# Feature sums and key-value sums in column tiles of 32, running states ahead of the linear masks

## The reference

```python
x = x + attn_a(layernorm(x), ...)   # stage a: 16 heads of 64
x = x + ffn(layernorm(x), ...)      # 16 experts, the best 8, and a shared one
x = x + attn_b(layernorm(x), ...)   # stage b: 6 transformer layers, 16 heads of 8
x = x + ffn(layernorm(x), ...)
```

```python
SK = jnp.cumsum(ok, axis=2) + SK_state[:, :, None]   # ok: kk (outer) vk, per token
norm = jnp.sqrt(jnp.sum(SK * SK, axis=(-2, -1), keepdims=True)) + 1e-08
y = jnp.einsum('bhni,bhnji->bhnj', q, SK / norm)
```

```python
kv = jnp.einsum('bhclm,bhcld->bhcmd', Kc, Vc)        # keys times values, per chunk
num = scores @ Vc + Qc @ (cumsum(kv) - kv)           # scores: masked Qc Kc^T
den = scores.sum(-1) + Qc @ (cumsum(ksum) - ksum)
```

## Time and profile before

| | |
|---|---|
| Time, median of 3 runs | 3790.42 us (3784.97 to 3793.73) |
| Time of the profiled execution | 3792.82 us |
| Its span, first to last instruction | 3791.1 us |
| Mean granted TensorE clock, share of full speed | 0.974 |
| Busy: PE, PEld | 3495.8 us (92%), 2727.7 us (72%) |
| Busy: DVE, ACT, POOL | 2686.2 us (71%), 1684.5 us (44%), 902.1 us (24%) |

### The profile page before, as it was taken

One profiled execution on the slowest core, in us unless ns is written; L12 is line 12 of the kernel. 1 busy time (PEld: TensorE's weight loads), 2 busy tenths in 40 slices (PEclk: granted clock), 3 DMA queues, 4 the chain that ended last, 5 costly groups with the idle time before them and its releaser, 6 DMA issues. The chain is left out here.

```text
span 3791.1 us, 98421 instructions
## 1 busy us (share of the span) xinstructions
PE 3495.8 (92%) x39640; PEld 2727.7 (72%) x39640; DVE 2686.2 (71%) x6838; ACT 1684.5 (44%) x3438; POOL 902.1 (24%) x781
## 2 busy tenths in 40 slices
PE   4999999999999999799948999999999999977998
PEld 3777777777777777688836777777777777756887
DVE  3666666666666666588866888878888888857787
ACT  2555555555555555433324444444444444423332
POOL 3222233222232322100002322332232223320000
PEclk9999999999999999899979999999999999988999
DMA  2000000000000000000000000000000000000000
GB/s 87 28 25 30 23 28 28 23 28 24 29 25 28 23 24 25 8 1 1 0 15 16 2 16 3 2 16 2 16 2 3 16 2 3 2 2 1 1 1 23
DMA packets 38361, 59.71 MB, mean 16 GB/s; under 512 B 6960, under 2 KB 16688, under 8 KB 37552
## 3 DMA queue, kind: packets, MB, share of 16 engines
q1 hardware_dynamic: 37936, 53.78, 4.2%
HBM read 18.10 MB, written 2.10 MB: 5 GB/s over the span
## 5 line engine op out<-in xcount | busy, mean ns | idle before, releaser
L661 ACT ACTIVATE a_prob<-a_s,a_shift,a_scale 128x128 f32<-128x128 f32 (+3 forms) x512 | 312.1, 614 | 531.1 <-DVE a_shift L744 531.1
L1541 ACT ACTIVATE ffn_silu<-ffn_ps_g 128x512 f32<-128x512 f32 x272 | 161.3, 599 | 383.5 <-PE ffn_ps_g L1491 371.6
L1484 PEld LDWEIGHTS ffn_ps_y<-moe_down,ffn_hidden 128*128 128x128 f32 x2176 | 282.1, 191 | 41.3 <-issue 19.9
L1484 PE MATMUL ffn_ps_y<-moe_down,ffn_hidden 128*128 128x128 f32 x2176 | 288.1, 275 | 17.4 <-DVE ffn_acc L1645 17.4
L943 POOL TENSOR_TENSOR t_rstd<-t_var_eps,minus_half 128x4 f32<-128x4 f32 x96 | 97.7, 1018 | 821.7 <-DVE t_var_eps L1255 821.7
L1193 ACT COPY t_num<-t_n 128x512 f32<-128x512 f32 x96 | 56.3, 586 | 517.9 <-PE t_n L1004 517.4
L1645 DVE SCALAR_TENSOR_TENSOR ffn_acc<-ffn_ps_y,ffn_combine,ffn_acc 128x128 f32<-128x128 f32 x960 | 269.4, 343 | 7.6 <-PE ffn_ps_y L1484 0.5
L1657 DVE TENSOR_TENSOR ffn_hidden<-ffn_silu,ffn_ps_u 128x512 f32<-128x512 f32 x272 | 185.1, 682 | 108.6 <-ACT ffn_silu L1541 74.6
L1330 DVE TENSOR_TENSOR t_mixed<-t_s,upto 128x512 f32<-128x512 f32 x384 | 238.1, 682 | 17.0 <-PE t_s L980 15.2
L408 POOL TENSOR_TENSOR a_k_sin<-a_k_swap,sin_swap 128x512 f32<-128x512 f32 x64 | 81.5, 1274 | 661.6 <-DMA a_k_swap<-a_k_own 661.6
L741 DVE TENSOR_REDUCE a_neg_max<-a_s 128x2 f32<-128x256 f32 (+3 forms) x256 | 208.8, 816 | 32.0 <-PE a_s L560 30.1
(11 more groups left out here) (209 smaller groups left out, 8777.3 us busy)
## 6 DMA issues: line engine op xcount, KB each, us to landing
a_k_swap<-a_k_own SPq DMA_DIRECT2D x128, 128.0 KB, 2.1
a_y_swap<-a_y_own SPq DMA_DIRECT2D x128, 128.0 KB, 2.0
a_staged<-in_pairs SPq DMA_DIRECT2D x8, 384.0 KB, 2.9
t_next<-in_t_w SPq DMA_DIRECT2D x12, 256.0 KB, 2.9
t_next_rows<-in_t_rows SPq DMA_DIRECT2D x6, 448.0 KB, 3.9
x<-in_x SPq DMA_DIRECT2D x8, 256.0 KB, 4.9
out<-x SPq DMA_DIRECT2D x1, 2048.0 KB, 8.7
t_next_sq<-in_t_sq SPq DMA_DIRECT2D x6, 256.0 KB, 2.5
```

Of the source, the lines that this page charges most:

```text
L661: nc.scalar.activation(prob[c % 2][h][:, 0:(c + 1) * P], ps[f"s{h}"][:, 0:(c + 1) * P], ACT.Exp, bias=shift[:, k:k + 1], scale=scale[slot. ...
L1484: t = nc.tensor.matmul(ps_y[e % 2][:, c * P:(c + 1) * P], hidden[e % 3][:, c * P:(c + 1) * P], w_down[:, e * P:(e + 1) * P], start=True, s ...
```

## The change

Four edits are made.

1. In stage a the step St moves ahead of L1 in DVE's order. PE's order, in which St already stands ahead of L1, stays.
2. The step inc is cut into column tiles: each of its 4 matmuls becomes 4, with 32 stationary columns each, written to 4 groups of 32 partitions.
3. In stage b the step sums is cut the same way: each of 8 matmuls with 128 stationary columns and 144 (or 72) streamed ones becomes 4 with 32 stationary columns and 36 (or 18) streamed ones, the 2 heads whose features those 32 columns are. All of it now fits in bank w0, and w1 is no longer used for it.
4. DVE's part follows: one copy and three adds on 72 (the last on 36) elements form the running sums in `k_sum`, from PSUM, and then two multiplications by `own_head` spread them into `kv`. Before, two such multiplications came first, from PSUM, and three adds on 288 (the last on 144) elements followed in `kv`.

The rest of the change is the declaration of the semaphores `k_sums` and `kv`, which replace `kv_sum`.

```diff
--- before.py
+++ after.py
@@ -215,7 +215,7 @@
     SLOT = ("P0 T3 S0 P1 W3 inv P2 S1 L0 outs T0 P3 weights T1 St L1 Xn S2 W0 W1 Yi Ys T2 S3 W2 inc").split()
     LEAD = "X P0 P1 P2 L0 P3 L1 Xn St Yi Ys inc".split()
     ACT = "P0 T3 S0 P1 inv P2 S1 T0 P3 T1 S2 Ys T2 S3".split()
-    DVE = "W3 S0 inv S1 L0 outs P3 weights L1 S2 St Ys S3 inc rot scale".split()
+    DVE = "W3 S0 inv S1 L0 outs P3 weights St L1 S2 Ys S3 inc rot scale".split()
     FILLS = dict(X="", Xn="", Yi="", P0="a0 a1", P1="a2 a0", P2="a1 a2", L0="a0 a1", P3="a0 a1", St="a2", L1="a0 a1",
                  Ys="a0 a1", inc="a2", inv="t0", outs="a2", T0="t0", weights="", T1="t1", T2="t0 t1", T3="t0 t1",
                  **{f"S{c}": "s0 s1" for c in range(TILES)},
@@ -523,8 +523,10 @@
                         wait(pe, "zk_sums", slot, 1)
                         free("a2")
                         for c in range(TILES):
-                            t = nc.tensor.matmul(ps["a2"][:, 2 * c:2 * c + 2], zk_upto[:, c * P:(c + 1) * P],
-                                                 mem["twos_own"][:], start=True, stop=True)
+                            for r in range(4):
+                                at = c * P + 32 * r
+                                t = nc.tensor.matmul(ps["a2"][32 * r:32 * (r + 1), 2 * c:2 * c + 2],
+                                                     zk_upto[:, at:at + 32], mem["twos_own"][:], start=True, stop=True)
                         t.then_inc(filled["a2"], 1)
                     elif step == "inv":
 
@@ -769,7 +771,7 @@
     END = "att Wo h1 F1 F2".split()
     DVE = "values Wo Wo_norm mapk keys weights F1 sums S0 F2 nums F2_norm S1".split()
     WITH = dict(Wo_norm="Wo", F2_norm="F2")
-    FILLS = dict(weights="", turn="w0", project="w1 w0", values="n1", mapq="s0 s1", mapk="s2 s3", keys="w0 w1", sums="w0 w1",
+    FILLS = dict(weights="", turn="w0", project="w1 w0", values="n1", mapq="s0 s1", mapk="s2 s3", keys="w0 w1", sums="w0",
                  S0="s0 s1 s2 s3", S1="s0 s1 s2 s3", A0="n0", A1="n1",
                  nums="w0 n1", att="n0", Wo="n0", h1="n0", F1="s0 s1 s2 s3", F2="w1")
 
@@ -792,7 +794,7 @@
     L, H, D, FEAT, FT = 6, 16, 8, 16, 4
     V = D + 1
     EPS = 1e-6 * FEAT
-    HALF = H // 2 * V
+    PAIR = 2 * V
     SPAN, SPANS = P // 2, 2 * TILES
     PAD = 16
     ROOT = float(D) ** -0.25
@@ -834,6 +836,7 @@
         k_tok = sb("k_tok", [P, 2, TILES, P])
         v_tok = sb("v_tok", [P, TILES, 2, H, V])
         v_pad = sb("v_pad", [P, SPANS, H // 2, 2, PAD])
+        k_sum = sb("k_sum", [P, 2, SPANS - 1, PAIR])
         kv = sb("kv", [P, SPANS - 1, H, PAD])
 
         mixed = [[sb(f"mixed{t}_{r}", [P, SPANS, SPAN]) for r in range(4)] for t in range(2)]
@@ -988,7 +991,7 @@
                     bank = f"n{t}"
                     if t == 0:
                         wait(pe, "v_pad", slot, 1)
-                        wait(pe, "kv_sum", slot, 3)
+                        wait(pe, "kv", slot, 2)
                     wait_free(pe, bank, slot, f"A{t}")
                     for r in range(4):
                         wait_free(pe, f"s{r}", slot, "A0" if t == 0 else slot.steps[0])
@@ -1057,17 +1060,20 @@
                     elif step == "sums":
 
                         wait(pe, "v_tok", slot, 1)
-                        for t_, bank in enumerate(("w0", "w1")):
+                        for bank in ("w0", "w1"):
                             ready(bank, "keys")
-                            free(bank)
+                        free("w0")
+                        for t_ in range(2):
                             for c in range(TILES):
                                 n = 2 if c < TILES - 1 else 1
-                                t = nc.tensor.matmul(
-                                    ps[bank][:, 2 * c * HALF:(2 * c + n) * HALF].rearrange("p (s n) -> p s n", s=n),
-                                    k_tok[:, t_, c, :],
-                                    v_tok[:, c, 0:n, 8 * t_:8 * t_ + 8, :].rearrange("p s h d -> p s (h d)"),
-                                    start=True, stop=True)
-                            t.then_inc(filled[bank], 1)
+                                at = (t_ * (SPANS - 1) + 2 * c) * PAIR
+                                for r in range(4):
+                                    t = nc.tensor.matmul(
+                                        ps["w0"][strip(r), at:at + n * PAIR].rearrange("p (s n) -> p s n", s=n),
+                                        k_tok[:, t_, c, strip(r)],
+                                        v_tok[:, c, 0:n, 8 * t_ + 2 * r:8 * t_ + 2 * r + 2, :]
+                                        .rearrange("p s h d -> p s (h d)"), start=True, stop=True)
+                        t.then_inc(filled["w0"], 1)
                     elif step == "S0":
 
                         wait(pe, "kz", slot, 2)
@@ -1292,24 +1298,25 @@
                             nc.vector.tensor_copy(k_tok[:, t_, :, :].rearrange("p c n -> p (c n)"),
                                                   ps[bank][:]).then_inc(emptied[bank], 1)
                     elif step == "sums":
-                        for t_, bank in enumerate(("w0", "w1")):
-                            full(bank)
+                        full("w0")
+                        new = ps["w0"][:, 0:2 * (SPANS - 1) * PAIR].rearrange("p (t s n) -> p t s n", t=2, n=PAIR)
+                        nc.vector.tensor_copy(k_sum[:, :, 0:2, :], new[:, :, 0:2, :]).then_inc(s["k_sums"], 1)
+                        for c in range(1, TILES):
+                            wait(dve, "k_sums", slot, c)
+                            at = slice(2 * c, min(2 * c + 2, SPANS - 1))
+                            n = at.stop - at.start
+                            t = nc.vector.tensor_tensor(k_sum[:, :, at, :], new[:, :, at, :],
+                                                        k_sum[:, :, 2 * c - 1:2 * c, :].broadcast_to([P, 2, n, PAIR]),
+                                                        ALU.add)
+                            t.then_inc(s["k_sums"] if c < TILES - 1 else emptied["w0"], 1)
+                        wait_emptied(dve, "w0", slot, "sums")
+                        for t_ in range(2):
                             nc.vector.tensor_tensor(
-                                kv[:, :, 8 * t_:8 * t_ + 8, 0:V],
-                                ps[bank][:, 0:(SPANS - 1) * HALF].rearrange("p (c h n) -> p c h n", c=SPANS - 1, h=8),
-                                mem["own_head"][:].rearrange("p (h n) -> p h n", h=8).unsqueeze(1)
-                                .broadcast_to([P, SPANS - 1, 8, V]),
-                                ALU.mult).then_inc(emptied[bank], 1)
-
-                        wait_emptied(dve, "w0", slot, "sums")
-                        wait_emptied(dve, "w1", slot, "sums")
-                        for c in range(1, TILES):
-                            if c > 1:
-                                wait(dve, "kv_sum", slot, c - 1)
-                            sums = kv[:, 2 * c:min(2 * c + 2, SPANS - 1), :, 0:V]
-                            n = sums.shape[1]
-                            nc.vector.tensor_tensor(sums, sums, kv[:, 2 * c - 1:2 * c, :, 0:V]
-                                                    .broadcast_to([P, n, H, V]), ALU.add).then_inc(s["kv_sum"], 1)
+                                kv[:, :, 8 * t_:8 * t_ + 8, 0:V].rearrange("p u (r h) n -> p u r h n", r=4),
+                                k_sum[:, t_, :, :].rearrange("p u (h n) -> p u h n", h=2).unsqueeze(2)
+                                .broadcast_to([P, SPANS - 1, 4, 2, V]),
+                                mem["own_head"][:].rearrange("p (r h n) -> p r h n", r=4, h=2).unsqueeze(1)
+                                .broadcast_to([P, SPANS - 1, 4, 2, V]), ALU.mult).then_inc(s["kv"], 1)
 
                         if "A1" in slot.steps:
                             wait_filled(dve, "n1", slot, "A1")
```

More of the change, by code:

```diff
@@ L857, in transformer_block @@
         emptied = {k: sem("emptied_" + k) for k in plan.BANKS}
-        EVENTS = dict(o_now=1, o_bias=1, kz=4, kv_sum=3, v_tok=1, v_pad=1, den=2, inv=2,
+        EVENTS = dict(o_now=1, o_bias=1, kz=4, k_sums=3, kv=2, v_tok=1, v_pad=1, den=2, inv=2,
                       stats=8, mv=8, eps=2, rstd=2, xn=8, scaled=2, h1b=1, o_new=1)
-        PHASE = {n: "in" if n in ("o_now", "kz", "kv_sum", "v_tok", "v_pad") else "mix" if n in ("den", "inv") else "out"
+        PHASE = {n: "in" if n in ("o_now", "kz", "k_sums", "kv", "v_tok", "v_pad") else "mix" if n in ("den", "inv") else "out"
                  for n in EVENTS}
@@ L1376, in _ @@
                 dve.sem_inc(made_out["dve"], 1)
-                begin(dve, "kv_sum stats mv eps xn den inv kz v_tok v_pad")
+                begin(dve, "k_sums kv stats mv eps xn den inv kz v_tok v_pad")
                 pipeline(dve, plan, weights_in, weights_out, body, plan.DVE)
```

## The result

The changed kernel takes 3724.72 us, the median of 4 runs (3718.72 to 3729.60), against 3789.68 us before: a ratio of 0.983, interval 0.9815 to 0.9842, or 65 us less. The forecast was 3705 us, in a range of 3686 to 3738. The profiled execution took 3718.72 us, 74 us less than that of before; it is the fastest of the four, so what is read from the two traces adds up to some 74 us and not to 65.

What follows compares the result with a forecast made beforehand. PE's own queue plus its waits bounds each slot, in stage a notably Ys waiting for the state. From the profiled 3792.8 us, less 42 (stage a), 44 (sums) and 2.4 to the median: 3705 us, range 3686 to 3738.

Steps and rivals of the forecast that it cites:

- adds within DVE's idle time: Stage a: moved state adds run from about 809.12 to 809.85, inside DVE's 1.37 us idle time ahead of L1's masks.
- 0.3 us of cover: Stage a: margin between the moved adds' end and L1's masks; were it gone, Yi would begin later.
- T2 in time: Stage a: T2's exponentials are through before 815.24, Ys ends near 815.4; about 0.2 us is left ahead of T2.
- the reason for the zero: Stage a: inc's 0.25 us a slot counts nothing, as T3's second half waits for exponentials whose chain doesn't pass through inc.
- S0 starts no earlier than 1.0 us behind: Stage b: S0 needs bank s3, emptied by DVE's second hid 0.95 us after sums starts; gain at most 0.96 us a slot.
- The pace of 14 ns: Start spacing of the new column-tile records, taken from A0's: sums 1.04 us with entry and end, 0.92 us saved a slot.
- 2.35 us forecast: Stage b: DVE's new running sums and two multiplications take 2.35 us instead of 3.0; A0 still does not wait.
- the 25 ns floor: Rival: records can't start within 25 ns of the last, sums takes 1.7 us, inc stays near 0.9; 3736 us, chance 10%.
- the moved stall: Rival, stage a: the adds or T2 hold PE up as Ys did, leaving only stage b's gain; 3746 us, chance 8%.
- the slower end: Rival: narrow tiles don't overlap, 0.048 us a record, so sums and inc get longer; 3851 us, chance 5%.
- Inc's saving getting through: Rival: T3 follows PE, so inc's shorter time counts, 16 to 20 us more; 3687 us, chance 7%.
- The clock: Main unseen risk within 4%: more and longer waits before T3 could bring 1.2 GHz stretches into stage a, granted clock 0.99.

Runs made afterwards that it cites:

- e4: The changed kernel with inc in its old form, without column tiles: 3720.59 us, ratio 0.9824 to the kernel before.
- e1: The kernel before with only the state adds moved ahead of L1's masks: 3749.83 us, ratio 0.9901.
- e9: The kernel before, with GpSimd's sum for the keys waiting for VectorE's third shift of the same slot: 3745.94 us, ratio 0.9883.
- e12: The kernel before with 34 unused semaphore increments per stage b slot (1024 instructions), 12 of them ahead of A1: 3812.80 us, ratio 1.0062.
- e13: The kernel before with GpSimd's wait for the third shift and 34 semaphore increments per stage b slot, all but four behind A1: 3715.15 us, ratio 0.9800.

## Why the prediction was right, and where it was off

The prediction took 86 us off, and 65 came. Stage a shrank by what it said and stage b by a third less; alone the two parts give 41 and 30 us, and the 6 us between their sum and 65 are within what these medians differ by (e4 has 70 us, and its interval of ratios overlaps with that of the changed kernel). (Its last step, 3706.8 less 2.4, is 3704.4 and not 3705, which changes nothing.)

**Edit 1, 42 us forecast:** e1 gave 41 us, and the stage shrank by 43 to 45. The working held: adds within DVE's idle time, 0.3 us of cover that sufficed, T2 in time. Its picture of the cause was half. It named the masks, the maximum and the shift as what stands ahead, and saw that the shift was long; e9 shows that without the shift's lost microsecond the masks and the maximum do no harm, and that one wait on GpSimd gives the same 45 us with the order left as it was.

**Edit 2, nothing forecast:** right by e4 against the changed kernel. The duration was off, since inc saves 0.55 us and not 0.25, but the reason for the zero, T3 behind the exponentials, is just what took it up: the wait of T3's weight load grew by 45.5 us, more than the 35 us saved, and the time of e4 is that of the changed kernel. That the tiles gain 8.6 us alone was not foreseen. It goes with the stall, met less often (52 to 39 waits): POOL's sum holds 34 of the shifts instead of 51. Why stays open. The swap of the keys, for which POOL waits, takes longer in more slots, 27 where it was 10, in 26 of them with an instruction packet in between; that was seen and not tried.

**Edits 3 and 4, 44 us forecast, 30 measured:** the mechanism was right and a term mis-sized. "S0 starts no earlier than 1.0 us behind" the start of sums allowed 0.05 us between the end of hid and S0; it is 0.25 us, of which semaphore instructions take most. And entering the tiling delays sums itself: F1 to sums takes 3.63 us, 3.54 before. Slots at good places went from 28.36 to 27.61 us, 0.75 instead of 0.92, or 36 us over 48. The remaining 6 us are the longer slots: the mean slot lay 0.88 us above the clean one before and 1.02 after. More gaps at page borders fit this, 36 for 28, with 96 instructions more in each slot, and the slow stretches behind gaps did not grow (58 us before, 51 after); that the 6 us are all due to borders is argued, not shown. The prediction had no term for either. The pace of 14 ns was too slow a guess (9 measured), but as the text said, S0's gate made that worth nothing.

**Edit 4:** 2.35 us forecast, 2.3 measured (2075.90 to 2078.21), and A0 hardly waits (3.5 us over the stage, in 2 slots). Each multiplication takes 0.64 us.

**The rivals:** the 25 ns floor (9 ns measured), the moved stall and the slower end fell with the first profile. Inc's saving getting through fell with e4. The clock, of which it feared slow stretches in stage a, stayed at 0.99 there.

## What to carry to other kernels

When a small instruction of VectorE is much longer than its like, look at what GpSimd runs beside it before reordering anything; one wait on the idle engine may be the whole repair. A form with more and smaller matmuls is to be priced by instructions too: where they follow each other at 7 to 15 ns, two page borders within some 3 us cost a gap of up to 1.3 us in the scores, and TensorE's clock may fall behind it, which costs again. If a loop's instruction count is brought near a multiple of 256, the borders stand still; then the start must be chosen, since a bad place is bad in every slot (e12), and a good one good in nearly all (40 of 45 in e13).

## What the runs showed of the hardware

- TensorE reads its program in pages of 256 instructions of 64 bytes. In the kernels before and after the change gaps of 0.2 to 1.6 us within the tiled groups stood at borders only, in S1 where the border before lay less than 2.8 us back. Some gaps in S0 came 5 to 9 us after the last border. In all 65 gaps of the two kernels an instruction packet ends 1.2 to 1.6 us before TensorE goes on; what delays it in S0 stays open.
- In the full slots of stage b, TensorE's clock fell to its lower level 15 times in the same two kernels, always 0.3 to 4.4 us behind such a gap.
- Matmuls in tiles of 128 x 32 with 36 or 18 columns start 9 ns apart, with their weight loads.
- With every semaphore ready, 0.37 us pass from the last matmul of one group to the first of the next where three semaphore instructions stand between them, 0.106 us from one of these to the next. Behind wide matmuls, 34 increments a slot did not lengthen the clean slots of stage b, 28.36 us with and without them.
- 54 of 256 two-column instructions of VectorE were lengthened, by up to 1.1 us, and none that began within an instruction of GpSimd ended before it.
